# Identity added on TensorE, residual evicted by ScalarE, and state products moved ahead of the first mask products

## The reference, cut to what matters

```
S = S * exp(gt)
kv = einsum('bhk,ebhkv->ebhv', kt, S)
delta = (vt - kv) * bt
S = S + kt[:, None] * delta[None, :]
o = einsum('bhk,ebhkv->ebhv', qt * scale, S)
```

## Time and profile before

| | before |
|---|---|
| time, median of 3 runs (lowest to highest) | 876.18 us (875.07 to 878.25) |
| the profiled execution's own time | 870.61 us |
| its span, first to last instruction | 868.7 us |
| mean granted TensorE clock | 0.986 of full speed |
| PE / DVE / ACT / POOL busy, share of the span | 92% / 74% / 36% / 34% |
| the chain that ended last | PE 63%, DVE 27%, issue 5% |

### The profile page before, as it was taken

One profiled execution on the slowest core, in us unless ns is written; L12 is line 12 of the kernel. 1 busy time (PEld: TensorE's weight loads), 2 busy tenths in 40 slices (PEclk: granted clock), 3 DMA queues, 4 the chain that ended last, 5 costly groups with the idle time before them and its releaser, 6 DMA issues.

```text
span 868.7 us, 23689 instructions
## 1 busy us (share of the span) xinstructions
PE 797.2 (92%) x10074; PEld 533.6 (61%) x10074; DVE 642.5 (74%) x1345; ACT 311.9 (36%) x547; POOL 292.7 (34%) x280
## 2 busy tenths in 40 slices
PE   2998999999999999999999996989999999897698
PEld 1453444444566647865444446888889898897343
DVE  7999999995888855534844547887878888773385
ACT  1231112210122230024544524646465565553342
POOL 5221110000111140000573335555656556551650
PEclk9999999999999999999999998999999999999899
DMA  8500000022000025000039643444545455421452
GB/s 249 195 0 1 0 2 1 0 49 71 2 1 1 1 70 198 0 1 1 4 97 406 254 143 109 135 138 126 156 127 146 130 140 148 129 61 39 126 176 72
DMA packets 74962, 80.47 MB, mean 93 GB/s; under 512 B 34453, under 2 KB 57671, under 8 KB 74854
## 3 DMA queue, kind: packets, MB, share of 16 engines
q1 hardware_dynamic: 69733, 57.78, 23.5%
q0 software_dynamic: 5120, 21.14, 6.7%
HBM read 54.44 MB, written 24.39 MB: 91 GB/s over the span
## 4 chain that ended last, share of the span: by engine, by line
PE 63%; DVE 27%; issue 5%; POOL 1%; ACT 1%; DMA 1%; SPq 1%; DVEq 0%; POOLq 0%; ACTq 0%
PE bank L786 14%; PE bank L854 7%; PE bank L1057 4%; DVE rows L1546 4%; PE bank L582 4%; PE bank L881 3%; PE bank L596 3%; DVE rows L1548 3%; PE bank L802 3%; DVE rows L1675 3%; PE bank L803 3%; PE bank L871 2%; PE bank L909 2%; PE bank L649 2%; PE bank L715 2%
## 5 line engine op out<-in xcount | busy, mean ns | idle before, releaser
L786 PE MATMUL bank<-W,xT 128*128 128x512 f32 x280 | 124.2, 596 | 0.7 <-ACT big L1136 0.7
L786 PEld LDWEIGHTS bank<-W,xT 128*128 128x128 f32 x280 | 52.0, 190 | 60.2 <-issue 57.9
L560 PE MATMUL bank<-W,xT 128*125 128x512 f32 x160 | 77.0, 595 | 0.0
L1375 POOL TENSOR_TENSOR cnt_r<-cnt_r,ident_sb 125x125 fp32r<-125x125 f32 x10 | 11.4, 1141 | 173.8 <-ACT cnt_r L1122 173.8
L582 PEld LDWEIGHTS bank<-rows 128*126 128x126 f16 x360 | 43.5, 135 | 34.7 <-issue 24.2
L1681 DVE TENSOR_SCALAR rows<-iota_sb,tC 128x625 f16<-128x625 f16 x180 | 56.2, 378 | 10.5 <-PE bank L582 10.5
L582 PE MATMUL bank<-rows 128*126 128x313 f16 x360 | 58.9, 299 | 4.2 <-DVE rows L1681 4.1
L1546 DVE TENSOR_SCALAR rows<-iota_sb,gbp 125x180 f16<-125x180 f16 x160 | 56.1, 351 | 0.0
L1548 DVE TENSOR_SCALAR rows<-iota_sb,gbp 125x180 f16<-125x180 f16 x160 | 50.2, 314 | 0.0
L1415 POOL TENSOR_TENSOR rows<-xn,masks_sb 128x512 f32<-128x512 f32 x20 | 26.2, 1309 | 71.2 <-DVE xn L1931 71.2
L570 PE MATMUL bank<-rows 125*128 125x360 f16 x160 | 42.7, 318 | 5.7 <-DVE rows L1548 3.3
(11 more groups left out here) (336 smaller groups left out, 1930.0 us busy)
## 6 DMA issues: line engine op xcount, KB each, us to landing
big<-qkv_slots SPq DMA_DIRECT2D x40, 256.0 KB, 3.4
rows<-step_rows SPq DMA_DIRECT2D x40, 128.0 KB
rows<-gam_rows SPq DMA_DIRECT2D x40, 128.0 KB
big<-qkv_slots SPq DMA_DIRECT2D x80, 64.0 KB, 2.6
big<-qkv_slots SPq DMA_DIRECT2D x40, 128.0 KB, 3.0
o_slots<-big SPq DMA_DIRECT2D x40, 128.0 KB, 2.9
x_all<-in_x SPq DMA_DIRECT2D x10, 224.0 KB
out<-tC SPq DMA_DIRECT2D x10, 224.0 KB
```

What stands on the lines that cost most here:

```text
L560: last = mm(dst, xT[:, k, t * P:(t + 1) * P], W[:, w, k, :], start=(k == 0), stop=(k == KC - 1 and bias is None))
L786: last = mm(bank[:, b0, :], xT[:, k, t * P:t * P + 128], W[:, w, k, :], start=(k == 0), stop=(k == KC - 1))
```

## The change

- A constant `eye16`, the identity twice over in f16, is made by one more ScalarE copy.
- TensorE's `residual` first writes the identity into the bank, with two f16 matmuls (one for each row half) of 64x64 weights and 512 columns, and then accumulates the products with `start=False`.
- ScalarE's `keep_t` writes `T0` with a scale of -1, so that the bank holds identity minus product.
- VectorE's `residual` is gone. ScalarE evicts the bank into `RES` by a new `keep_residual`, which stands ahead of `keep_mt`; the former `keep_residual` is now `keep_residual16` and stays behind `keep_mt`.
- On TensorE `state_part` of the first chunk stands ahead of `first_m`; on VectorE `new_state` of the first chunk stands ahead of `level_b` 1.

```diff
+        eye16 = sb("eye16", [128, CL], f16)
...
                 pe.wait_ge(S["ati_done"], u + 1)
                 pe.wait_ge(S["t_done"], u + 1)
-                products(MB[s], AT[s], T0).then_inc(S["res_psum"], 1)
+                for b in range(2):
+                    q = slice(CL * b, CL * b + CL)
+                    mm(bank[q, MB[s], :], eye16[q, :], bm(eye16[q, :], 8), start=True, stop=True, skip_group_check=True)
+                products(MB[s], AT[s], T0, lambda a: False).then_inc(S["res_psum"], 1)
...
                 unit_of(residual, h - 1)
+                chunk_of(state_part, h, 0)
                 unit_of(first_m, h)
-                chunk_of(state_part, h, 0)
                 unit_of(first_mt, h)
...
             A(pairs16[:, :], level0T, ACT.Copy).then_inc(S["ln_table"], 1)
+            A(eye16[:, :], eye64, ACT.Copy).then_inc(S["ln_table"], 1)
...
-                A(flat(T0), bank[:, TB[s], :], ACT.Copy).then_inc(S["t_done"], 1)
+                A(flat(T0), bank[:, TB[s], :], ACT.Copy, scale=-1.0).then_inc(S["t_done"], 1)
...
             def keep_residual(u):
+                act.wait_ge(S["res_psum"], u + 1)
+                A(flat(RES), bank[:, MB[u % 2], :], ACT.Copy).then_inc(S["res_done"], 1)
+
+            def keep_residual16(u):
                 act.wait_ge(S["res_done"], u + 1)
                 A(RES16, RES, ACT.Copy).then_inc(S["uu_done"], 1)
...
                 chunk_of(keep_z, h, 0)
+                unit_of(keep_residual, h - 1)
                 unit_of(keep_mt, h)
-                unit_of(keep_residual, h - 1)
+                unit_of(keep_residual16, h - 1)
...
-            def residual(u):
-                s = u % 2
-                dve.wait_ge(S["res_psum"], u + 1)
-                V.tensor_tensor(RES, bm(eye64, 8), pm(MB[s]), ALU.subtract).then_inc(S["res_done"], 1)
...
                 unit_of(scores, h)
-                unit_of(residual, h - 1)
+                chunk_of(new_state, h, 0)
                 unit_of(level_b, h, 1)
-                chunk_of(new_state, h, 0)
                 unit_of(level_b, h, 2)
```

## The result

The changed kernel takes 879.40 us (median of 20 runs, 876.17 to 883.63) against 876.53 us (median of 20, 874.12 to 879.13): a ratio of 1.0030, 95% interval 1.0019 to 1.0041. It is 2.9 us slower at the medians, measurable though under 0.5%. 879.4 lies in the range of 872.8 to 880.0, near its upper end, and outside the 873.8 to 878.8 of the forecast case alone. The two traces alone therefore show more than the medians do; only what they share with the repeated runs counts.

A forecast was written before the change was run, and what follows sets the result against it. TensorE, busy 92% of the span, was taken to bound the kernel. Losses of 1.8 us and gains of 1.7 us gave net +0.1 us on 876.18 us: 876.3 us, range 872.8 to 880.0.

The forecast's parts named there:

- the forecast case alone: Whole kernel: time nearly unchanged, 873.8 to 878.8 us; chance 0.62, counted together with first_mt not being held by the scores.
- The identity pair at 0.22 us: TensorE's residual step: two identity products on the two row halves side by side add 0.22 us a unit.
- the rival of 0.43 us: TensorE's residual step: identity products run one after the other, 0.43 us a unit, 879.2 us; chance 0.18, alone or with borders.
- Subtraction and eviction at nothing: VectorE losing the residual's subtraction (0.60 us of queue) gains nothing; ScalarE's eviction (0.60 us) ahead of keep_mt costs nothing.
- The moves' gain, capped at 0.26 us a unit by the scores: TensorE's mask products: state products fill first_m's wait, but first_mt needs VectorE's scores, so at most 0.26 us a unit.
- the new one in about seven units: TensorE's first_mt weight load would wait for VectorE's scores in about seven units; a sign of being right.
- The sum: TensorE over the recurrence: losses of 1.8 us against gains of 1.7 us, net +0.1 us.
- the unit stay at 13.6 us: Recurrence: the average unit would stay at 13.6 us; a sign of being right.
- The term of the issue stalls: TensorE in the recurrence: moved code borders show up to five stalls more or fewer, 0.5 us each, plus or minus 2.5 us.

The follow-up runs named there:

- rows of 408: Kernels with 408 matmuls a unit (kernel before, moves alone, no identity, shifted forms of the first two), grouped by border place: ratios 0.9987 to 1.0048.
- kernels of 410: Kernels with 410 matmuls a unit; cited are the changed kernel shifted by 16 one-column matmuls (1.0011), unshifted (1.0030) and shifted by 31 (1.0064).
- the two moves alone shifted by 31: Kernel before with only the two moves, and 31 one-column matmuls ahead of the recurrence: 874.78 us, ratio 0.9987.
- experiment 8: Changed kernel with one identity product of 128 partitions in place of the two of 64: 879.74 us, ratio 1.0035 to the kernel before.

## Why the prediction was right, and which step was off

- **The identity pair at 0.22 us** is right to the hundredth, and the rival of 0.43 us fell (743.49 to 743.71), although its 879.2 us came closest to the time. A number that fits is no evidence for its mechanism.
- **Subtraction and eviction at nothing** is right: without the identity the ratio is 0.9996.
- **The moves' gain, capped at 0.26 us a unit by the scores.** The cap is real in the code and seldom binds: 3 waits, 0.5 us. The steps became 0.4 us a unit shorter by the moves alone, where the cap had allowed 0.26. TensorE now comes late enough for transposes and scores to be done. The wait went, as forecast, but the new one in about seven units didn't come.
- **The sum is the step that failed.** It added up TensorE's time in the steps, as if a shorter step made a shorter unit. The moves alone shortened the steps by 0.4 us a unit and the time by nothing; the identity's 0.22 us brought down to 0.04 left the cost where it was. Nor did the unit stay at 13.6 us: the profiled loop gives 14.0. The time of this loop is set to a good part by the borders, which come every 256 instructions, some 125 matmuls, and by when the code behind them arrives.
- **The term of the issue stalls**, 2.5 us either way around a sum of +0.1, is what decided: of its size, and of the sign that I had left open. +2.9 at the medians is a little more than it. That the time lies in the range is owed to this spread, which was a guess from the number of stalls, and not to the sum: that is luck in part. Also right was that the change moves every border. It gives each unit 410 matmul instructions in place of 408 and so changes how the borders drift through the units.

The Trainium skill, "Runtime: NRT & Kernel Launch", section "Instruction fetch mechanics", says that the cost of crossing a 16 KiB border is mostly hidden. In this loop it is hidden at just over half of the borders only: 397 of 903 end in a printed stall, 12.8 to 22.7 us in an execution, and the same loop differs by 4 to 5 us by their place alone.

**What stays open.** Why a packet starts 1.5 us behind a border in some steps and 2.5 in others isn't shown. The loads that run beside the loop may have a part in this; it wasn't tried. The length of the run alone doesn't decide: in the kernel before, 8 of the 9 runs under 3.35 us ended in a stall and 2 of the 10 from 4.05 to 4.3 us, but over all fourteen traces it is 43 of 78 and 69 of 143. The order in the rows of 408 is clear; among the kernels of 410 no such order shows (1.0011, 1.0030, 1.0064). And the old order with the identity (1.0071) is slower than the new one with it (1.0030) at the same place, while without the identity the two are equal.

No version beats the kernel before clearly. The best, the two moves alone shifted by 31, has 0.9987 (0.9972 to 1.0002), and that isn't told from no change.

## What to carry to other kernels

When an engine works through unrolled code back to back, look at its "issue" stalls before you count what a shorter step brings: if they come at a fixed spacing of instructions, the gain may be given back at the next border, and four instructions more can cost more than the work they do. Before you believe a change of half a per cent in such a kernel, shift the code by a few dozen idle instructions, in the old kernel as in the new one, and compare the best places of both. An explanation that fits one time should be made to pay with its time taken out and its instructions left in.

## What the runs showed of the hardware that wasn't expected

- Two f16 matmuls of 64x64 weights and 512 columns on the two halves of the array take 0.22 us together from start to start.
- Sixteen matmuls of one column ahead of a loop of 260 us made it 4 us slower in one kernel (1.0048) and 2 us faster in the other (1.0030 to 1.0011); thirty-one made the first one equal to the original (0.9991) and the second one slower (1.0064).
- One product of 128x128 weights and 512 columns takes 0.32 us at the same place (experiment 8), a tenth of a us more than the pair.
- TensorE's issue stalls stand at every 256th of its instructions, weight loads and semaphore instructions counted (392 of 405 within 8 instructions behind it), and end 1.1 to 1.7 us after a 16 KB packet of the instruction queue has landed. That queue moved 82 packets in each of the fourteen executions.
